# Spectral mixer on Trainium2: inverse transform laid out by image, its last stage on eight 32x64 tiles

## The chip, the cores and the metric

One core of a Trainium2 chip runs the whole kernel in one launch. The metric is device time in microseconds, the median of the runs shown. The engines are TensorE (PE), VectorE (DVE), ScalarE (ACT), GpSimd (POOL) and SyncE (SP), which here only issues transfers.

## The reference, cut to what matters

Input: x of shape (2, 64, 64, 384): two images, 64 rows (h), 64 columns (w), 384 channels. Four layers of the same kind follow each other; the second one is wrapped in a layer norm and followed by a two-layer token MLP with a second layer norm.

```python
xf = rfft2(x, axes=(1, 2))                   # 64 x 33 complex frequencies
o1 = act(complex_linear(xf, w1) + b1)        # 8 blocks of 48 channels; relu, or gelu in layer 1
o2 = complex_linear(o1, w2) + b2
o2 = softshrink(o2, 0.01)                    # layers 0, 2, 3
y  = irfft2(o2, s=(64, 64)) + x
# layer 1: ln -> the same with xk = xf[:, :32, :32], the rest zero -> + x -> ln -> gelu MLP -> + residual
```

Layers 0, 2 and 3 keep all 64 x 33 frequencies ("full" layers); layer 1 (the "norm" layer) keeps 32 x 32.

## The kernel before, in words

The work is done in 32 blocks, numbered g: layer g // 8, 48 channels each, so block g of a layer has one of its 8 channel groups. Two blocks are a unit (96 channels), which is what SP loads and stores; three buffers `xs` hold units. Partition of `xs` is (image, w). Blocks run in three segments: 0 to 7 (layer 0), 8 to 15 (layer 1, then the token MLP) and 16 to 31 (layers 2 and 3). Within a segment the stages of neighbouring blocks overlap, in an order written out by hand, in slots t: a full block has 9 slots (groups of 6 or 8 frequency slots), a norm block 4.

Stages of a block:
- `f1` (L479): transform along w, on 64x64 tiles of the array, three calls of 32 matmuls per block. Its input `xn` is turned by POOL (L1160). ACT copies the results into `z` (L726), four pieces per call.
- `f2` (L509): transform along h, ACT copies it into `zf` (L744). `m1` and `m2` (L527, L541): the two mixing matmuls, with ACT's activation `h` (L769) between them. In full layers DVE clamps and subtracts the result of `m2` into `u` (L931, L937), four subtractions per slot, one for each image and real or imaginary part.
- `f5` (L570): inverse along h, six calls (k = 0 to 5) per block, bank 5 of the PSUM alone, ACT copies it into `v` (L790).
- `f6` (L592): inverse along w, eight calls per block, each for 8 rows of the image: two matmuls with all 128 partitions of `v` (real or imaginary, frequency, image) as the contraction, 64 output columns each, 384 moving columns. The basis is zero where the image of the row isn't that of the output. DVE adds the result to the residual in `xs` (L954), 128x384 at a time, and in layer 0 takes `bn_stats` of every row there (L974), of 96 channels on odd blocks and of 48 on the last two.

Frequency 32, the last of the 33, needs only its real part, and frequency 0 needs no imaginary one: `f5` reads `u` shifted by one frequency for the imaginary half, so that frequency 32 lies where frequency 0's imaginary part would. For the norm layer two memsets on POOL (L1232) clear that place.

Order in slot t of block g on PE, full layers (L607): m1(g, t-1), f2(g, t), one f6 call (rows t+1 of block g-2; at t = 8 row chunk 0 of block g-1), f1(g+1) at t = 0, 3, 6, f5(g-1) at t = 2 to 7, m2(g, t-1). ACT (L804) and DVE (L1008) have orders to match. Each engine runs its own order strictly; they meet in semaphores. `f6` waits for `v_ready` (all six parts of `v`) and `res_ready` (the adds that free its bank). `m2` waits for `h_ready` and for the subtractions of the group two before it. At a segment's end PE finishes the rest without new blocks (L643 to L654).

SP stores a unit in four parts of 16 rows for each image when `res_ready` tells that both blocks' rows are there (L370), and then loads the next unit into the buffer. ACT and POOL issue no transfers.

Of the kernel before, what the change touches and what calls it, by code (L numbers as in the profile page):

```python
# [33 lines left out]
PIECES = ((0, 0), (0, 1), (1, 1), (1, 0))  # L34
ROWCHUNK = 8
# [5 lines left out]
AHEAD = 3  # L41
# [5 lines left out]
C_ID, C_D5, C_D5H, C_D6, C_COLS = [C_SIGN + SIGNS + P * n for n in range(5)]  # L47
# [11 lines left out]
class Layer:  # L59

    def __init__(self, index, kh, forward, inverse, act, shrink, norm):
        self.index, self.kh, self.forward, self.inverse = index, kh, forward, inverse
        self.act, self.shrink, self.norm = act, shrink, norm
        self.full = kh == SIDE
        self.spread = 2 * BATCH if self.full else BATCH
        self.first_rows = 1 if self.full else 0
# [47 lines left out]
def drains(g, k):  # L114

    last = [b for _, b in SEGMENTS if g < b][0]
    return g == last - 1 or g == last - 2 and k >= layer_of(g).first_rows


ROW_CHUNKS = [(g, k) for g in range(LAYERS * BLOCKS) for k in range(ROWCHUNKS)]  # L120


def row_bank(g, k):
    return 1 if drains(g, k) and k % 2 else 0


def rows_to_clear(g, k):

    n = ROWCHUNKS * g + k
    earlier = [m for m in range(n) if row_bank(*ROW_CHUNKS[m]) == row_bank(g, k)]  # L130
    return earlier[-1] + 1 if earlier else 0
# [63 lines left out]
def build(nc, x, consts, spectral, lncols, ln1, cols, w1, w2, b2, out):  # L195
    with ExitStack() as ctx:
# [24 lines left out]
        power = sb("power", [P, 1])  # L221
        eps = sb("eps", [P, 1])
# [4 lines left out]
        with ExitStack() as scope:  # L227
# [10 lines left out]
            u = sb("u", [P, 2, BLOCK, SPAN + BATCH])  # L238
# [3 lines left out]
            v = sb("v", [P, 2, SIDE, BLOCK])  # L242
# [31 lines left out]
        F1_BANKS, M2_BANKS, F6_BANKS = (0, 1), (4, 7), (6, 0)  # L274
        F2_BANK, M1_BANK, F5_BANK = 2, 3, 5
        LAST_BANKS = (F5_BANK, M1_BANK)
# [9 lines left out]
        f5_done, f6_done = sem("f5_done"), sem("f6_done")  # L286
        z_ready, zf_ready, h_ready = sem("z_ready"), sem("zf_ready"), sem("h_ready")
        clamped, u_ready, v_ready = sem("clamped"), sem("u_ready"), sem("v_ready")
        res_ready, gap_clear, u_clear = sem("res_ready"), sem("gap_clear"), sem("u_clear")
# [22 lines left out]
        TURN_AT = 8  # L312

# [5 lines left out]
        def residual(g, first, rows):  # L319

            n = g % 2
            return xs[buffer_of(g // 2)][:, first:first + rows, n * BLOCK:(n + 1) * BLOCK]
# [154 lines left out]
        def _(pe):  # L477

            def f1(g, k):  # L479
# [17 lines left out]
                if leads(g) and g and k == 1:  # L497
                    pe.wait_ge(res_ready, ROWCHUNKS * g)
                for c in range(CHAN):
# [41 lines left out]
            def m2(g, t):  # L541
# [9 lines left out]
                if L.full:  # L551
                    for c in range(size):
# [17 lines left out]
            def f5(g, k, bank=F5_BANK, reuse=1):  # L570
# [3 lines left out]
                if k == 0:  # L574
# [5 lines left out]
                    if L.norm and g % BLOCKS < 2:  # L580
                        pe.wait_ge(u_clear, 2)
                if n >= reuse:
                    pe.wait_ge(v_ready, n + 1 - reuse)
                for c in range(CHAN):
                    for a in range(2):
                        mm = pe.matmul(ps[a * SIDE:(a + 1) * SIDE, bank, c * SIDE:(c + 1) * SIDE],  # L586
                                       u[:, g % 2, k * CHAN + c, BATCH * a:BATCH * a + SPAN],
# [4 lines left out]
            def f6(g, k):  # L592

                n = ROWCHUNKS * g + k
                if k == 0:
                    pe.wait_ge(v_ready, CHUNKS * (g + 1))
                clear = rows_to_clear(g, k)
                if clear:
                    pe.wait_ge(res_ready, clear)
                rows = slice(k * ROWCHUNK, (k + 1) * ROWCHUNK)  # L600
                for a in range(2):
                    mm = pe.matmul(ps[a * SIDE:(a + 1) * SIDE, F6_BANKS[row_bank(g, k)], 0:ROWCHUNK * BLOCK],  # L602
                                   basis(C_D6 + a * SIDE, SIDE), v[:, g % 2, rows, :].rearrange("p h c -> p (h c)"),
                                   start=True, stop=True)
                mm.then_inc(f6_done, 1)

            def spectral(first, last):  # L607
# [3 lines left out]
                for g in range(first, last):  # L611
                    L = layer_of(g)
                    for t in range(L.n):
# [4 lines left out]
                        rows = [r for r in rows_at(g, t) if r[0] >= first]  # L618
                        ahead = at_slot(L.f1_at, t) if g + 1 < last else []
                        behind = at_slot(L.f5_at, t) if g > first else []  # L620
                        if not L.full:
                            for r in rows[0:1]:
                                f6(*r)
                        f2(g, t)
                        if L.full:
                            for r in rows:
                                f6(*r)
                            for k in ahead:
                                f1(g + 1, k)
                        for k in behind[0:1]:  # L630
                            f5(g - 1, k)
                        if not L.full:
                            for r in rows[1:]:
                                f6(*r)
                            for k in ahead:
                                f1(g + 1, k)
                        for k in behind[1:]:
# [3 lines left out]
                        elif g > first:  # L641
                            m2(g - 1, layer_of(g - 1).n - 1)
                g = last - 1  # L643
                m1(g, layer_of(g).n - 1)
                for k in range(L.first_rows, 4):
                    f6(g - 1, k)
                m2(g, layer_of(g).n - 1)
                f6(g - 1, 4)
                for k in range(CHUNKS):
                    if k < 3:  # L650
                        f6(g - 1, 5 + k)
                    f5(g, k, LAST_BANKS[k % 2], 2)
                for k in range(ROWCHUNKS):
                    f6(g, k)  # L654
# [69 lines left out]
        def _(act):  # L724
# [53 lines left out]
            def m2(g, t):  # L778
# [5 lines left out]
                for b in range(BATCH):  # L784
                    part = slice(SIDE + b * HALF, SIDE + (b + 1) * HALF)
                    act.activation(u[HALF:SIDE, g % 2, :, start + b:start + size:BATCH],
                                   ps[part, bank, 0:size // BATCH * BLOCK].rearrange("p (s c) -> p c s", c=BLOCK),
                                   ACT.Copy).then_inc(u_imag, 1)

            def f5(g, k, bank=F5_BANK):  # L790

                act.wait_ge(f5_done, CHUNKS * g + k + 1)
                if k == 0 and g >= 2:
                    act.wait_ge(f6_done, ROWCHUNKS * (g - 1))
                act.activation(v[:, g % 2, :, k * CHAN:(k + 1) * CHAN],
                               ps[:, bank, :].rearrange("p (c h) -> p h c", h=SIDE), ACT.Copy,
                               scale=layer_of(g).inverse).then_inc(v_ready, 1)

# [5 lines left out]
            def spectral(first, last):  # L804
# [5 lines left out]
                for g in range(first, last):  # L810
                    L = layer_of(g)
                    for t in range(L.n):
# [3 lines left out]
                        if L.full:  # L816
                            for k in late:
# [5 lines left out]
                        if not L.full:  # L823
                            for k in late:
                                f1(g + 1, k, PIECES[2:4])
# [6 lines left out]
                        for k in behind[0:1]:  # L832
                            f5(g - 1, k)
                        if not L.full:
                            for k in ahead:
                                f1(g + 1, k, PIECES[0:1])
                        for k in behind[1:]:
                            f5(g - 1, k)
                        if not L.full:
                            for k in ahead:  # L840
# [496 lines left out]
```

## Time and profile before

| | us |
|---|---|
| median of 3 runs (2064.65 to 2067.0) | 2065.68 |
| span of the profiled execution, first to last instruction | 2057.0 |
| median less span (launch and end) | 8.7 |
| PE busy, share of the span | 93% |
| DVE, ACT, POOL busy | 57%, 49%, 21% |

The page gives the profiled execution by its span alone; its own time from outside is not shown, so the median stands beside it. The segments lie in the span as follows: blocks 0 to 7 from 28 to 357 us, blocks 8 to 15 to 631 us, the token MLP to about 1460 us, blocks 16 to 31 to the end.

How to read it: a group of matmuls is told by its line. An fp32 matmul has two LDWEIGHTS and two MATMUL records. A busy time is the union of the records; the chain of waits cuts the same time into pieces that don't overlap. "issue" is time for which the profile shows no waiting.

### The profile page before, as it was taken

What the parts mean: (1) busy time and instruction counts of PE and PEld (TensorE: products, weight loads), DVE (VectorE), ACT (ScalarE), POOL (GpSimd) and SP (SyncE); (2) the same over time, 40 slices, a digit from 0 to 9 for tenths busy, and PEclk for the clock granted to TensorE, in tenths of its full rate; (3) what the DMA queues carried; (4) which work ended last, traced back from release to release, by engine and by line L of the source; (5) the groups of instructions that cost most, each with busy time, mean ns of one, the idle gap of its engine ahead of it and who ended that gap; (6) DMA issues with size and microseconds to landing.
All of it is one profiled execution on the core that took longest, in us unless ns stands there. A gap on an engine that the chain in (4) does not pass through costs nothing.

```text
span 2057.0 us, 68971 instructions
## 1 busy us (share of the span) xinstructions
PE 1919.2 (93%) x31104; PEld 1570.9 (76%) x31104; DVE 1173.7 (57%) x2480; ACT 1008.7 (49%) x1644; POOL 435.4 (21%) x425
## 2 busy tenths in 40 slices
PE   4999995698998999999999999999899999999996
PEld 3777772576776999999999999999777777777774
DVE  3687887977855433333333333332377767677675
ACT  3766545576753333333333333333466666665652
POOL 3212104965631000000000000000221211221200
PEclk9999997799999999999999999999999999999998
DMA  9425738307434111111111111114532573557314
GB/s 164 100 49 85 129 62 142 55 4 129 114 86 122 32 31 31 31 31 31 31 31 31 31 31 31 31 31 73 94 53 49 87 127 80 84 99 126 60 40 96
DMA packets 299701, 141.05 MB, mean 69 GB/s; under 512 B 275760, under 2 KB 298032, under 8 KB 299440
## 3 DMA queue, kind: packets, MB, share of 16 engines
q1 hardware_dynamic: 299440, 137.08, 36.2%
q8 instruction: 224, 3.67, 0.8%
q14 instruction: 37, 0.30, 0.1%
HBM read 74.14 MB, written 62.91 MB: 67 GB/s over the span
## 4 chain that ended last, share of the span: by engine, by line
PE 80%; DVE 9%; SPq 3%; ACT 2%; issue 2%; POOL 2%; DMA 1%; DVEq 0%; POOLq 0%; ACTq 0%
PE ps L693 20%; PE ps L678 19%; PE ps L586 8%; PE ps L523 8%; PE ps L537 7%; PE ps L602 6%; PE ps L555 5%; PE ps L504 4%; DVE u L937 3%; DVE st L974 2%; SPq L357 1%; DVE xs L962 1%; PE ps L565 1%; DMA wraw<-in_w 1%; PE ps L663 1%
## 5 line engine op out<-in xcount | busy, mean ns | idle before, releaser
L1086 DVE TENSOR_TENSOR gl<-g,gh 128x512 fp32r<-128x512 f32 x192 | 156.8, 816 | 476.3 <-ACT gh L872 476.3
L937 DVE TENSOR_TENSOR u<-ps,clamp 64x192 f32<-64x192 f32 (+1 forms) x864 | 378.1, 438 | 27.7
L869 ACT ACTIVATE g<-ps,colp 128x512 f32<-128x512 f32 x192 | 132.3, 689 | 529.1 <-PE ps L678 529.1
L523 PEld LDWEIGHTS ps<-const,z 128*48 128x48 f32 x8384 | 266.0, 124 | 134.9 <-issue 128.6
L732 ACT ACTIVATE z<-ps 64x512 f32<-64x512 f32 x366 | 234.9, 642 | 155.1 <-PE ps L504 148.2
L523 PE MATMUL ps<-const,z 128*48 128x64 f32 (+1 forms) x8384 | 270.3, 217 | 10.2 <-issue 5.3
L1173 POOL COPY xn<-xs 128x512 f32<-128x512 f32 x144 | 152.0, 1096 | 535.8 <-PE ps L504 343.9
L693 PE MATMUL ps<-w2h,gh 128*128 128x384 f32 x768 | 261.9, 341 | 0.0
L693 PE MATMUL ps<-w2h,gl 128*128 128x384 f32 x768 | 258.6, 337 | 0.0
L693 PE MATMUL ps<-w2l,gh 128*128 128x384 f32 x768 | 257.5, 335 | 0.0
L586 PEld LDWEIGHTS ps<-const,u 128*64 128x64 f32 x6144 | 206.7, 139 | 52.2 <-issue 25.7
L537 PE MATMUL ps<-zf,w 112*64 112x512 f32 (+1 forms) x992 | 244.2, 566 | 1.3 <-ACT zf L758 0.9
L602 PE MATMUL ps<-v,const 128*64 128x384 f32 x1024 | 216.1, 500 | 22.5 <-DVE xs L962 20.2
L586 PE MATMUL ps<-const,u 128*64 128x64 f32 x6144 | 220.0, 225 | 15.2 <-DVE u L942 7.6
L678 PE MATMUL ps<-mth,w1h 128*128 128x512 f32 x576 | 224.9, 390 | 4.0 <-DVE mtl L1074 4.0
L775 ACT ACTIVATE h<-ps,w 113x512 f32<-113x512 f32 (+1 forms) x248 | 162.7, 656 | 133.3 <-PE ps L537 130.8
L678 PE MATMUL ps<-mth,w1l 128*128 128x512 f32 x576 | 228.0, 396 | 0.0
L678 PE MATMUL ps<-mtl,w1h 128*128 128x512 f32 x576 | 227.6, 395 | 0.0
L931 DVE TENSOR_SCALAR clamp<-ps 128x384 f32<-128x384 f32 (+1 forms) x216 | 112.6, 521 | 181.6 <-PE ps L555 180.7
L504 PEld LDWEIGHTS ps<-const,xn 64*64 64x64 f32 x6144 | 110.0, 146 | 105.7 <-issue 77.9
L504 PE MATMUL ps<-const,xn 64*64 64x64 f32 x6144 | 124.3, 234 | 61.1 <-POOL xn L1173 23.5
L555 PE MATMUL ps<-w,h 113*64 113x96 f32 x3168 | 173.7, 248 | 7.4 <-ACT h L775 5.0
(70 smaller groups left out, 2463.4 us busy)
## 6 DMA issues: line engine op xcount, KB each, us to landing
after<-xs SPq DMA_DIRECT2D x96, 384.0 KB, 5.4
xs<-after SPq DMA_DIRECT2D x94, 384.0 KB, 8.8
after<-om SPq DMA_DIRECT2D x32, 384.0 KB, 4.3
out<-xs SPq DMA_DIRECT2D x32, 384.0 KB, 5.5
xm<-after SPq DMA_DIRECT2D x30, 384.0 KB, 6.3
xs<-in_x SPq DMA_DIRECT2D x24, 384.0 KB, 8.4
wstage<-in_spectral SPq DMA_DIRECT2D x16, 210.0 KB, 5.8
xs<-in_x SPq DMA_DIRECT2D x4, 768.0 KB, 11.9
```

The source lines that it names most:

```text
L504: mm = pe.matmul(ps[j * SIDE:(j + 1) * SIDE, banks[b], c * SPAN:(c + 1) * SPAN], xn[rows, slot, first + j, :], const[rows, C_D1:C_D1 + SPA ...
L523: mm = pe.matmul(ps[a * SIDE:a * SIDE + BLOCK, F2_BANK, n * L.kh:(n + 1) * L.kh], z[:, g % 2, slot, :], basis(col + a * SIDE, L.kh), start ...
L537: mm = pe.matmul(ps[rows, M1_BANK, 0:width], w[unit % 2][0:MIX, g % 2, rows], zf[0:MIX, n % 2, 0:width], start=True, stop=True)
L555: mm = pe.matmul(ps[b * SIDE:(b + 1) * SIDE, bank, p * PAIR:(p + 1) * PAIR], h[0:ROWS, n % 2, c * SIDE:(c + 1) * SIDE], mix[0:ROWS, g % 2, ...
L586: mm = pe.matmul(ps[a * SIDE:(a + 1) * SIDE, bank, c * SIDE:(c + 1) * SIDE], u[:, g % 2, k * CHAN + c, BATCH * a:BATCH * a + SPAN], basis( ...
L602: mm = pe.matmul(ps[a * SIDE:(a + 1) * SIDE, F6_BANKS[row_bank(g, k)], 0:ROWCHUNK * BLOCK], basis(C_D6 + a * SIDE, SIDE), v[:, g % 2, rows ...
L678: mm = pe.matmul(ps[:, MM1_BANKS[n % 2], :], a[:, at], b[r][:, k, :], start=k == 0 and m == 0, stop=k == KC - 1 and m == 2)
L693: mm = pe.matmul(ps[:, MM2_BANKS[j], 0:CHANNELS], a[:, n % 4, part], b[:, at], start=n == 0 and m == 0, stop=n == HC - 1 and m == 2)
L732: act.activation(to, data, ACT.Copy, scale=layer_of(g).forward).then_inc(z_ready, 1)
L775: act.activation(h[0:ROWS, n % 2, 0:width], ps[0:ROWS, M1_BANK, 0:width], L.act, bias=w[g // 2 % 2][0:ROWS, g % 2, READY_BIAS:W_ALL]).then ...
L937: dve.tensor_tensor(u[to, g % 2, :, start + b:start + size:BATCH], whole, limited, ALU.subtract).then_inc(u_ready, 1)
L1086: dve.tensor_tensor(gl[:, n % 4, :], g[:, n % 2, :], gh[:, n % 4, :], ALU.subtract).then_inc(g_low, 1)
```

## The change

`u` and `v` get the image as an outer index and the channels in two halves of 24 (TWO): `u[h part, parity, image, t, half, frequency]`, `v[..., image, row, t]`. The partition of `v` becomes (real or imaginary, channel half, frequency), four groups of 32. `f6` becomes two bursts of 32 rows per block, each on four banks: in step 0 all four 32-partition groups times two images run, each on its own 32x64 tile of the array; step 1 adds the other part (imaginary for real) into the same banks, after a semaphore `f6_half` that the last matmul of step 0 raises. Burst 0 of block g-1 stands at slot 8 of block g, burst 1 of block g-2 at slot 1 (both at slot 0 of the norm blocks). `f1` moves to slots 2, 4, 6, and `f5` to 2, 3, 4, 5, 6, 6 with two banks. Frequency 32 gets its own tile `last`, four small subtractions, a small `f5_last` (two matmuls at slot 2 of the next block, one DVE operation), and four transfers that ACT issues at the head of slot 7, each of 64 partitions x 96 bytes into one partition of `v`; burst 0 waits for them. The POOL memsets go.

```diff
-        self.f1_at = [0, 3, 6] if self.full else [0, 1, 2]
-        self.centre_at = [0, 0, 1, 2, 2, 3]
-        self.f5_at = [2, 3, 4, 5, 6, 7] if self.full else [1, 1, 2, 2, 3, 3]
+        self.f1_at = [2, 4, 6] if self.full else [1, 2, 3]
+        self.centre_at = [0, 1, 1, 2, 3, 3]
+        self.f5_at = [2, 3, 4, 5, 6, 6] if self.full else [1, 1, 2, 2, 3, 3]
-def rows_at(g, t):
+def bursts_at(g, t):
     if not layer_of(g).full:
-        return [(g - 2, 2 * t), (g - 2, 2 * t + 1)]
-    if t == layer_of(g).n - 1:
-        return [(g - 1, 0)]
-    return [(g - 2, t + 1)] if t < ROWCHUNKS - 1 else []
+        return [(g - 2, r) for r in range(BURSTS)] if t == 0 else []
+    return {1: [(g - 2, 1)], layer_of(g).n - 1: [(g - 1, 0)]}.get(t, [])
+STATS_AT = {0: (0, 1), 2: (2,), 3: (3,), 4: (4,), 5: (5,), 6: (6,), 7: (7,)}
+        BURST_BANKS, LAST_BURST_BANKS = (*F1_BANKS, *F5_BANKS), (M1_BANK, *M2_BANKS, F1_BANKS[0])
...
+            def f5_last(g):
+                pe.wait_ge(last_ready, 2 * BATCH * full_before(g + 1))
+                bank = last_bank(g)
...
+                for b in range(BATCH):
+                    mm = pe.matmul(ps[b * SIDE:(b + 1) * SIDE, bank, LAST_AT:LAST_AT + BLOCK],
+                                   basis(C_D5 + SIDE, SIDE), last[:, g % 2, b, :], start=True, stop=True)
+                mm.then_inc(last_done, 1)
...
+            def f6(g, r):
...
+                if r == 0:
                     pe.wait_ge(v_ready, CHUNKS * (g + 1))
+                    if layer_of(g).full:
+                        pe.wait_ge(v_whole, LAST_MOVES * full_before(g + 1))
+                    if g + 1 == last:
+                        pe.wait_ge(res_ready, ROWCHUNKS * g)
+                    elif layer_of(g).full:
+                        pe.wait_ge(z_ready, z_before(min(g + 3, last)))
+                elif g + 1 == last:
+                    pe.wait_ge(res_ready, ROWCHUNKS * g + 1)
+                else:
+                    pe.wait_ge(res_ready, ROWCHUNKS * g + 4)
+                for step in range(2):
+                    if step:
+                        pe.wait_ge(f6_half, BURSTS * g + r + 1)
+                    for n, bank in enumerate(burst_banks(g, r)):
+                        part, half = n // 2, n % 2
+                        a = part ^ step
+                        quadrant = slice((2 * a + half) * HALF, (2 * a + half + 1) * HALF)
+                        rows = slice(r * BURST_ROWS + part * BURST_PART, r * BURST_ROWS + (part + 1) * BURST_PART)
+                        for b in range(BATCH):
+                            mm = pe.matmul(ps[b * SIDE:(b + 1) * SIDE, bank, 0:BURST_PART * TWO],
+                                           const[quadrant, column:column + SIDE],
+                                           v[quadrant, g % 2, b, rows, :].rearrange("p h c -> p (h c)"),
+                                           start=step == 0, stop=step == 1)
+                    mm.then_inc(f6_done if step else f6_half, 1)
...
+            def place_last(g):
+                act.wait_ge(v_ready, CHUNKS * (g + 1))
+                act.wait_ge(last_kept, full_before(g + 1))
+                for b in range(BATCH):
+                    for j in range(2):
+                        row = SIDE + j * HALF
+                        act.dma_start(v[row:row + 1, g % 2, b], turned_last[b * SIDE:(b + 1) * SIDE, g % 2, j * TWO:(j + 1) * TWO]
+                                      ).then_inc(v_whole, 16)
...
+                        if start + size > SPAN:
...
+                            dve.tensor_tensor(last[to, g % 2, b, :], whole, limited, ALU.subtract).then_inc(last_ready, 1)
...
+            def f6(g, r):
...
+                dve.wait_ge(f6_done, BURSTS * g + r + 1)
+                for n, bank in enumerate(burst_banks(g, r)):
+                    to = residual(g, r * BURST_ROWS + n // 2 * BURST_PART, n % 2)
+                    dve.tensor_tensor(to, ps[:, bank, 0:BURST_PART * TWO].rearrange("p (h c) -> p h c", c=TWO),
+                                      to, ALU.add).then_inc(res_ready, 1)
...
-            pool.wait_ge(f5_done, CHUNKS * BLOCKS)
-            for n in range(2):
-                pool.memset(u[0:SIDE, n, :, SPAN:], 0.0).then_inc(u_clear, 1)
```

## Rows read from the trace of the kernel before

**Rows 1.** The page: busy time of the engines; the chain that ended last, by line.

```profile
PE 1919.2 (93%) x31104; PEld 1570.9 (76%) x31104; DVE 1173.7 (57%) x2480; ACT 1008.7 (49%) x1644; POOL 435.4 (21%) x425
...
PE ps L693 20%; PE ps L678 19%; PE ps L586 8%; PE ps L523 8%; PE ps L537 7%; PE ps L602 6%; PE ps L555 5%; PE ps L504 4%; DVE u L937 3%; DVE st L974 2%; SPq L357 1%; DVE xs L962 1%; PE ps L565 1%; DMA wraw<-in_w 1%; PE ps L663 1%
```

**Rows 2.** Busy time by stretch (us, then each engine): a block of layer 0, one with statistics, one of layer 2, a norm block.

```profile
93.83:128.34 34.51, 34.51 (x850) 25.85 (x848) 24.81 (x56) 22.02 (x37) 8.30 (x12) 1.00 0.01 3
128.34:163.71 35.37, 35.00 (x848) 25.88 (x844) 33.68 (x113) 22.08 (x36) 6.45 (x6) 1.00 0.47 96
1570.84:1605.41 34.57, 34.57 (x850) 25.88 (x848) 24.85 (x54) 22.09 (x36) 6.38 (x6) 1.00 0.51 102
432.70:460.71 28.01, 27.68 (x818) 21.21 (x816) 25.75 (x30) 21.33 (x35) 21.92 (x18) 1.00 0.02 4
```

**Rows 3.** Chain of waits, pieces of blocks 20 and 30 (start, us, what, records).

```profile
1612.91 0.93 PE ps L586 x32
...
1616.26 0.65 PE ps L602 x4
1616.90 1.09 PE ps L504 x64
1617.99 1.08 PE ps L586 x32
1619.08 0.66 PE ps L555 x16
1619.74 0.86 PE ps L537 x4
...
1993.13 0.67 PE ps L523 x24
```

**Rows 4.** Groups of PE by shape: f5 and f6 (busy, mean ns of a record, idle before).

```profile
L586 PE MATMUL ps<-const,u 128*64 128x64 f32 x6144 | 220.0, 225 | 15.2 <-DVE u L942 7.6 <-issue 3.0 <-ACT v L795 2.9
...
L602 PE MATMUL ps<-v,const 128*64 128x384 f32 x1024 | 216.1, 500 | 22.5 <-DVE xs L962 20.2 <-ACT v L795 2.1
```

**Rows 5.** Timeline of ACT, the same slots (start, us, what, idle before).

```profile
1618.06 1.30 ACT L732 ACTIVATE z<-ps 64x512 f32<-64x512 f32 x2 [1.16 <-PE ps L504]
1619.38 0.60 ACT L795 ACTIVATE v<-ps 128x512 f32<-128x512 f32 x1
1620.01 0.63 ACT L732 ACTIVATE z<-ps 64x512 f32<-64x512 f32 x1
1620.66 0.69 ACT L775 ACTIVATE h<-ps,w 113x512 f32<-113x512 f32 x1
```

**Rows 6.** Issues of SP by line, ns min/median/max: the smallest ones.

```profile
L392 SPq DMA_DIRECT2D wraw<-in_w x6: 327/328/432, 60.9 to 83.5; - x6
L464 SPq DMA_DIRECT2D lncol<-in_lncols x1: 437/437/437, 60.0 to 60.0; - x1
```

**Rows 7.** The same: a load of a unit's rows, four parts of two images each.

```profile
L357 SPq DMA_DIRECT2D xs<-after x96: 592/1981/3574, 236.4 to 1897.8; - x96
```

**Rows 8.** Transfers: KB each and median us from issue to landing.

```profile
const<-in_consts SPq DMA_DIRECT2D x1, 32.0 KB, 1.8
lncol<-in_lncols SPq DMA_DIRECT2D x1, 8.0 KB, 4.8
```

**Rows 9.** Groups of DVE by shape: subtractions, residual adds, row statistics.

```profile
L937 DVE TENSOR_TENSOR u<-ps,clamp 64x192 f32<-64x192 f32 x576 | 282.3, 490 | 18.5
...
L962 DVE TENSOR_TENSOR xs<-ps,xs 128x384 f32<-128x384 f32 x256 | 141.5, 554 | 54.7 <-PE ps L602 49.3
...
L974 DVE BATCH_NORM_STATS2 st<-xs 128x6 f32<-128x96 f32 x192 | 33.1, 246 | 0.8
```

**Rows 10.** Timeline of the end: last f6 calls, adds and stores.

```profile
2037.65 6.09 PE L602 MATMUL ps<-v,const 128*64 128x384 f32 x32 [0.70 <-ACT v L795]
...
2038.57 1.20 DVE L962 TENSOR_TENSOR xs<-ps,xs 128x384 f32<-128x384 f32 x2 [4.74 <-PE ps L602]
...
2039.80 12.46 SPq L375 DMA_DIRECT2D out<-xs  x8
```

More of the change, by code:

```diff
@@ L34 @@
 PIECES = ((0, 0), (0, 1), (1, 1), (1, 0))
+BURST_ROWS, BURST_PART = 32, 16
+BURSTS = SIDE // BURST_ROWS
 ROWCHUNK = 8
@@ L111, in imag_of, with segment_of, full_before @@
     return sum(BATCH for g, _ in GROUPS[:count] if layer_of(g).norm)
[L114 to L131, printed above, removed]
+def segment_of(g):
+    return [segment for segment in SEGMENTS if segment[0] <= g][-1]
+def full_before(g):
+    return sum(layer_of(n).full for n in range(g))
 def shrunk_before(g):
@@ L551, in m2 @@
                 if L.full:
+                    if t == LAST_SLOT and g > segment_of(g)[0]:
+                        f5_last(g - 1)
                     for c in range(size):
@@ L590, in f5 @@
                 mm.then_inc(f5_done, 1)
-            def f6(g, k):
-                n = ROWCHUNKS * g + k
-                if k == 0:
+            def f6(g, r):
+                first, last = segment_of(g)
+                column = C_D6 if layer_of(g).full else C_D6 + SIDE
+                if r == 0:
                     pe.wait_ge(v_ready, CHUNKS * (g + 1))
[L597 to L605, printed above, removed]
+                    if layer_of(g).full:
[22 more added lines that the diff above has]
+                    mm.then_inc(f6_done if step else f6_half, 1)
@@ L617, in spectral @@
                             m1(g - 1, layer_of(g - 1).n - 1)
-                        rows = [r for r in rows_at(g, t) if r[0] >= first]
+                        bursts = [r for r in bursts_at(g, t) if r[0] >= first]
                         ahead = at_slot(L.f1_at, t) if g + 1 < last else []
@@ L621, in spectral @@
                         if not L.full:
[L622 to L627, printed above, removed]
                             for k in ahead:
                                 f1(g + 1, k)
[L630 to L634, printed above, removed]
+                        f2(g, t)
+                        for r in bursts[0:1]:
+                            f6(*r)
+                        if L.full:
                             for k in ahead:
                                 f1(g + 1, k)
-                        for k in behind[1:]:
+                        for k in behind:
                             f5(g - 1, k)
@@ L816, in spectral @@
                         if L.full:
+                            if t == L.f5_at[-1] + 1 and g > first:
+                                place_last(g - 1)
                             for k in late:
@@ L831, in spectral @@
                                 f1(g + 1, k, PIECES[0:2])
-                        for k in behind[0:1]:
+                        else:
+                            for k in ahead:
+                                f1(g + 1, k, PIECES[2:4])
+                        for k in behind:
                             f5(g - 1, k)
[L834 to L840, printed above, removed]
-                                f1(g + 1, k, PIECES[1:2])
                         if L.norm and t:
@@ L926, in m2 @@
                 if L.full:
+                    if t == LAST_SLOT and g > segment_of(g)[0]:
+                        f5_last(g - 1)
                     pairs = size // BATCH
```

204 lines of the change are left out of this document (122 added, 82 removed).

## The prediction, made before the changed kernel ran

> **What bounds the kernel now.** I read the page first. PE is busy for 1919 of 2057 us and the chain that ended last is almost all PE [rows 1]. The token MLP's two lines hold 39% of it; the change doesn't touch them. f6 (L602) holds 6%, f5 8%, f2 8%. The busy share is a mean over stages, so I read single blocks next. In a clean full block PE is busy for all of its 34.5 us, DVE for 24.8, ACT for 22.1; in a block of layer 0 with row statistics DVE is up to 33.7 of 35.4; in a norm block PE has 27.7 and DVE 25.8 of 28.0 us [rows 2]. So PE's own work sets the pace of the full layers, with DVE just behind it where there are statistics and in the norm layer. The chain's pieces give the price of each stage on PE without overlap: one f6 call 0.65 us, f5 0.93, m2 0.66, m1 0.86, f2 of six slots 0.67, f1 1.09 [rows 3]. f6 is 8 x 0.65 = 5.2 us of each block. Most blocks away from the ends of a segment run like this.
>
> **What tiles cost and give.** f5's 32 records take 0.93 us on two tiles; f1's 64 records of the same 64 columns take 1.09 on four. That is 0.93 for twice as many records plus 0.16, and the f5 behind it takes 1.08, again 0.15 more [rows 3]. So four tiles run side by side, and each change of the tile shape costs 0.15 us. A f6 call streams 384 columns with two records per tile: 0.325 us a record. A record itself lasts about 0.49 without waits (the mean of 500 ns holds some slow ones) [rows 4], so a result is ready 0.16 us after its stream ends.
>
> **The bursts.** A burst has 16 matmuls in two steps of eight, one for each tile. If all eight run side by side it streams for 2 x 0.325 = 0.65, plus 0.05 for starting eight. Step 1 waits for the end of step 0: 0.16 for the last results, and some 0.12 for the semaphore and for loading weights that could not be loaded ahead, an estimate from the 0.15 of a shape change, which is a drain of the same kind. A burst then costs 0.15 + 0.70 + 0.28 + 0.70 + 0.15 = 1.98 us, two of them 3.96 against 5.2: 1.24 us less per full block. The trace shows no 32-row tile, so bounds: if nothing is paid between the steps 1.7 a burst (-1.8 per block); if only four of the eight tiles run at once each step is 1.35 and a burst 3.3 (+1.4 per block). I take 1.98, because f1 shows full use of all tiles there are.
>
> A page of the Trainium skill speaks against this. "TensorE: Matmul & The Clock Gate", section "Part 3: Packing small matmuls — row/col tiling", says that matmuls start and end in strict program order. By that rule the second record of a tile would hold back the next tile, and a step would take 2.9 us where I take 0.70. Were it so in f1, its 64 records could not end in 1.09 us; it is a rival below.
>
> **f5_last and the split subtractions.** f5_last is four records of 48 columns; m2's 16 of 96 take 0.66 [rows 3], so about 0.1 on PE. Net of f6 and this: -1.14 per full block. DVE gets four more small subtractions in one slot and one small copy, about 0.7 us per block between 64x192's 0.49 and nothing [rows 9]; it has 9.7 us to spare in a clean block [rows 2]: free. New write patterns in u (runs of four words in place of every second word) could make the 0.49 us shorter or longer; DVE is not the pace there: free. Two banks for f5 take away a wait that is small already (idle before f5 15.2 us in all, little of it for v) [rows 4]. The POOL memsets lie beside other work: nothing.
>
> **The four transfers on ACT.** Here the change pays. ACT issues them at the head of slot 7, after its last v copy, and everything behind them on ACT's queue comes later: one z piece and, above all, h for m2(6). PE at that point: from the end of the last f5 it has m2 0.66, m1 0.86, f2 0.67 = 2.19 us until it wants that h. ACT, by rows of the same kind: v done about 0.8 after f5 ends (a start 0.2 after it, then 0.60), z 0.63, h 0.69 = 2.15 [rows 5]. So the cover is 0.04 us and the time of the four issues falls on PE in full. Nothing before gives ACT's issue time. SP's smallest are 0.33 (wraw) and 0.44 us (lncol, 128 short rows) [rows 6]; these have 64 short rows. Bounds: 0.15 (half the smallest row, since the rows are half as many) and 2.0, what an issue of SP takes with its queue full [rows 7]. I take 0.40, nearest to lncol in kind: 1.6 us per block. Then the landing: small transfers landed after 1.8 us on an idle queue and 4.8 behind others [rows 8]. Between ACT's last issue and burst 0 PE does m2, m1, f2 and waits for h: z 0.63 + h 0.69 + m2 0.66 + m1 0.7 + f2 0.67 = 3.35 us. At 1.8 it is hidden; at 4.8 it costs 1.5. I take hidden.
>
> **Who waits for the bursts.** DVE adds four tiles of 0.55 us in a row [rows 9], 2.2 us, and a m2 group behind them. At slots 8, 0 and 1 DVE has two such bursts and three groups of m2, each four subtractions of 0.33 to 0.49 us (six slots have three quarters of the elements) and a clamp of about an add's 0.5: some 10.5 us, and PE about 10; m2 may run two groups ahead and f1 has moved from slot 0 to 2, where banks 0 and 1 are free just in time. Nothing in clean blocks. In blocks of layer 0 with statistics the new order puts 16 bn_stats (0.17 us each: 33.1 for 192) into slot 0: 2.7 us more, of which I count 2 as stall, in blocks 3, 5 and 7.
>
> **Norm blocks.** Both bursts stand in slot 0, with a m2 between them (32 records, about 0.9 like f5's); burst 1 waits for the adds of burst 0, 2.2 us: a stall of 1.3. Then 2 x 1.98 + 1.3 = 5.3, what f6 costs now. DVE is at 92% of such a block anyway. I count 0 per block, between -2 and +2.
>
> **Ends.** Segment 3 ends with f6, then SP's eight stores of 1.56 us each and a landing [rows 10]. Now place_last stands bare in front of f6: 1.6 + 1.8 = 3.4 us, and the first two adds come 0.9 later than now (a whole burst first). Fewer waits in the drain of the block before give 1.3 back: +3. The end of layer 0 is a DVE queue (statistics), 0; the end of the norm layer gains about 1.5 because two f6 calls no longer stand between the f5.
>
> **The sum.** Layers 2 and 3: 16 x -1.14 + 15 x 1.64 = +6.4; end +3. Layer 0: 8 x -1.14 + 7 x 1.64 + 3 x 2 = +8.4, of which part is covered by DVE; I take +5. Norm 0 and -1.5. Together +13 us against the span of 2057.0; the median of the runs shown lies 8.7 above that span. So 2065.7 + 13 = 2079.
>
> **The rivals.** (A) The transfers are cheap or hidden: issue 0.15, or ACT's queue goes on beside it. Then the place costs at most 0.64 per block, the net is -0.5 to -1.1, and layers 0, 2 and 3 give 24 x -0.5 to -1.1, with the same ends and statistics stalls down to 2: 2041 to 2060, about 2048. For it: 64 rows only, an empty queue. Against: no issue under 0.33 in the trace. The point from which it decides is four issues in 1.1 us. (B) Issuing is slow while SP's queue is full: 2.0 us each in the blocks where SP loads, every second one, for 11 blocks: 11 x 6.4 = +70 on the forecast, 2150; half of that at 1.2 us, 2110. For it: SP's median of 1.98. Against: that may be the filling of its own ring. (C) The eight tiles don't run side by side, four do: 4 x 0.65 = +2.6 per block over my sum in 32 blocks, +83, 2160. So the change would not do what it says. Against: f1's four tiles. (D) Records start in strict order, so a tile's second record holds back the next tile: a step takes (8 + 1) x 0.325 = 2.93 in place of 0.70, 4 x 2.2 = +9 per block, 32 blocks, +285, 2364. Only f1's row bears on it, against it. Slower by another way than my forecast are B, C, D; A ends on the other side.
>
> **Chances.** Forecast 0.41 (its own range 2065 to 2098), A 0.36, B 0.13, C 0.07, D 0.03. 0.2% is 4 us, about what a measurement of this kernel tells from no change. Faster by more: A's most, 0.32. Within it: 0.12, the upper end of A and the lower of the forecast. Slower: 0.56. The range for 8 in 10 reaches from A's 2040 over the forecast to B's lower case with the landing bare, 2125; it leaves out half of B, C, D and A's low end (all bounds at their good end, 24 x -1.4: 2032).
>
> **What would show it.** In the profile after: per burst 32 records of 128 rows' worth in 32x64 tiles, from first to last start about 1.7 us; f6 below 140 us of PE. ACT's 96 DMA issues at 0.3 to 0.5 us; a new wait of PE for ACT's h of about 1.6 us once per full block; hardly any wait of f6 for a DMA outside the last block. Clean full block 34.5 -> 35.0 us; if it is 33.4 to 34, A holds; if f6 keeps over 3 us a burst, C or D. The prediction is wrong if the norm blocks change by over 2 us each, or if DVE turns into the releaser of PE in clean blocks.

## The result, and the profile of the changed kernel

The changed kernel takes 2148.65 us (median, 2144.1 to 2157.1), the kernel before beside it 2065.16 (2061.5 to 2067.0): ratio 1.0404, 95% interval 1.0373 to 1.0435. I had said 2079, at most 2125. The direction was right, the size was not: +83.5 us where +13 was forecast.

The page of the changed kernel, its span 2155.3 us: the first two lines answer to those of [rows 1], the third is the group of m2 on PE:

```profile
PE 1925.4 (89%) x32224; PEld 1572.0 (73%) x32224; DVE 1162.0 (54%) x2608; ACT 1004.2 (47%) x1644; POOL 442.8 (21%) x423
...
PE ps L740 19%; PE ps L725 19%; PE ps L544 8%; PE ps L622 8%; PE ps L558 7%; PE ps L578 6%; PE ps L653 5%; PE ps L525 5%; ACTq L854 2%; DVE xs L1032 2%; SPq L376 1%; DVE xn L1069 1%; PE ps L710 1%; DVE u L1000 1%; DVE st L1047 1%
...
L578 PE MATMUL ps<-w,h 113*64 113x96 f32 x3168 | 182.5, 255 | 56.1 <-ACT h L822 49.3
```

PE does 6 us more than before, and the span is 98 us longer: PE waits. Half of the wait has a name, ACT's h in front of m2 (L578), 49.3 us where it was 5.0 before. The same by stretch (columns as in [rows 2]): a clean block of layer 0, one with statistics, a block with loads, a clean block, and the 15 blocks 16 to 30 together:

```profile
100.22:136.59 36.37, 33.77 (x886) 25.54 (x886) 24.34 (x60) 22.12 (x36) 8.38 (x12) 1.00 0.02 4
136.59:174.43 37.84, 33.96 (x886) 25.82 (x886) 35.25 (x124) 22.12 (x36) 6.43 (x6) 1.00 0.55 113
1770.91:1812.63 41.72, 36.84 (x886) 27.35 (x886) 24.22 (x60) 22.06 (x36) 6.34 (x6) 0.92 0.90 160
1971.32:2007.69 36.37, 33.76 (x886) 25.54 (x886) 23.86 (x59) 22.11 (x36) 8.35 (x12) 1.00 0.02 4
...
1504.13:2083.32 579.19, 521.08 (x12958) 392.51 (x12958) 354.69 (x844) 327.85 (x535) 101.75 (x121) 0.96 0.43 75
```

The same 15 blocks, and two of them (24 with loads, 25 with stores alone), in the kernel before:

```profile
1475.56:1993.86 518.30, 507.07 (x12458) 384.34 (x12460) 361.46 (x772) 327.11 (x535) 101.61 (x121) 1.00 0.48 83
...
1746.81:1783.62 36.81, 35.15 (x850) 26.58 (x848) 24.85 (x54) 22.02 (x37) 8.33 (x12) 1.00 0.54 83
1783.62:1818.18 34.56, 34.56 (x850) 25.87 (x848) 24.87 (x54) 22.05 (x36) 6.41 (x6) 1.00 0.50 102
```

A clean block went from 34.5 to 36.37 us, a block with loads from 36.8 to 41.7, and in the latter the granted clock fell to a mean of 0.92 of full. So there are two losses, one in each block and one beside SP's transfers. The first stands in the chain of waits of block 28, slots 6 to 8 (start, us, what):

```profile
1997.13 0.61 ACT v L843
...
1997.76 0.47 ACTq L854
1998.23 0.03 issue
1998.26 0.62 ACTq L854
...
2000.17 0.05 issue
2000.22 0.63 ACT z L779
...
2000.88 0.70 ACT h L822
2001.57 0.04 issue
2001.62 0.88 PE ps L578 x16
...
2003.82 0.92 PE ps L653 x16
2004.73 0.04 issue
2004.77 0.91 PE ps L653 x16
```

Four issues on ACT's queue reach from 1997.76 to 2000.17, 2.42 us, and z, h and m2 come behind them. The burst, whose price was the least certain, is as worked out: its two steps take 0.92 + 0.04 + 0.91 = 1.87 us. The individual records of this burst show its first eight starts within 0.05 us of each other, and the second record of each tile 0.37 us later: eight tiles side by side. Issue durations (ns min/median/max) and landing, by line:

```profile
L854 ACTq DMA_DIRECT2D v<-turned_last x96: 470/618/1522, 90.2 to 2131.9; - x96
...
DMA to landing us min/median/max: 1.7/1.9/7.2
```

The group of f6 on PE (busy, mean ns of a record, idle before); it was 216.1 us busy in [rows 4]:

```profile
L653 PE MATMUL ps<-v,const 32*64 32x384 f32 x2048 | 132.7, 570 | 37.8 <-DVE xs L1032 15.8 <-issue 13.3 <-ACT v L843 0.7
```

### The profile page after: what moved, and what is told of

Read it like the earlier page. It is cut to its first block, busy times and chain, and to the rows that moved or that the text cites. A ratio compares the mean times of both kernels' runs of the same rounds, so it can differ in the third digit from the quotient of the medians.

```text
span 2155.3 us, 71501 instructions
## 1 busy us (share of the span) xinstructions
PE 1925.4 (89%) x32224; PEld 1572.0 (73%) x32224; DVE 1162.0 (54%) x2608; ACT 1004.2 (47%) x1644; POOL 442.8 (21%) x423
## 4 chain that ended last, share of the span: by engine, by line
PE 79%; DVE 7%; issue 4%; ACT 3%; SPq 3%; ACTq 2%; POOL 1%; DMA 0%; DVEq 0%; POOLq 0%
PE ps L740 19%; PE ps L725 19%; PE ps L544 8%; PE ps L622 8%; PE ps L558 7%; PE ps L578 6%; PE ps L653 5%; PE ps L525 5%; ACTq L854 2%; DVE xs L1032 2%; SPq L376 1%; DVE xn L1069 1%; PE ps L710 1%; DVE u L1000 1%; DVE st L1047 1%
## 5 line engine op out<-in xcount | busy, mean ns | idle before, releaser
L544 PEld LDWEIGHTS ps<-const,z 128*48 128x48 f32 x8384 | 276.3, 128 | 142.3 <-issue 134.2
L1000 DVE TENSOR_TENSOR u<-ps,clamp 64x192 f32<-64x192 f32 (+2 forms) x864 | 365.1, 423 | 24.6
L544 PE MATMUL ps<-const,z 128*48 128x64 f32 (+1 forms) x8384 | 283.7, 222 | 17.1 <-issue 12.1
L558 PE MATMUL ps<-zf,w 112*64 112x512 f32 (+1 forms) x992 | 257.9, 592 | 5.0 <-issue 2.0
L578 PE MATMUL ps<-w,h 113*64 113x96 f32 x3168 | 182.5, 255 | 56.1 <-ACT h L822 49.3
L622 PE MATMUL ps<-const,u 128*64 128x64 f32 x6144 | 215.0, 227 | 15.6 <-issue 11.0
L622 PEld LDWEIGHTS ps<-const,u 128*64 128x64 f32 x6144 | 198.2, 141 | 22.2 <-issue 13.2
L578 PEld LDWEIGHTS ps<-w,h 113*64 113x64 f32 x3168 | 145.7, 140 | 92.3 <-ACT h L822 57.1
```

What stands on the lines that cost most here:

```text
L544: mm = pe.matmul(ps[a * SIDE:a * SIDE + BLOCK, F2_BANK, n * L.kh:(n + 1) * L.kh], z[:, g % 2, slot, :], basis(col + a * SIDE, L.kh), start ...
L558: mm = pe.matmul(ps[rows, M1_BANK, 0:width], w[unit % 2][0:MIX, g % 2, rows], zf[0:MIX, n % 2, 0:width], start=True, stop=True)
L578: mm = pe.matmul(ps[b * SIDE:(b + 1) * SIDE, bank, p * PAIR:(p + 1) * PAIR], h[0:ROWS, n % 2, c * SIDE:(c + 1) * SIDE], mix[0:ROWS, g % 2, ...
L1000: dve.tensor_tensor(modes(g, to, b, start, size), whole, limited, ALU.subtract).then_inc(u_ready, 1)
```

## Experiments: the transfers

The first four runs separate the transfers from the new order of PE's work.

```diff
e1   -    place_last(...)   and the waits on v_whole
e2   -    for b, for j: act.dma_start(v[row, g % 2, b], ...)        4 x 64 rows of 96 B
     +    for j:        act.dma_start(v[row, g % 2], turned_last[:, g % 2, j])   2 x 128 rows
e3   as e2, but pool.dma_start behind POOL's six turns of a block
e4   kernel before, plus 4 x act.dma_start(spare, turned_last) at the head of slot 7
```

**e1**, expected:

> The changed kernel without the four transfers that ACT issues per full block and without the waits for them (frequency 32 is still computed, but not placed). Theory A (the issues stand on PE's path through ACT's queue, about 2.5 us per full block, and the gaps let TensorE's clock fall): a clean full block goes from 36.4 to about 33.9 us, 24 blocks give 60 us, the clock and the fetch stalls behind the gaps up to 30 more: 2055 to 2090 us, no PE wait for h over 0.5 us. Theory B (the bursts and the new order of the slots cost the time, the transfers little): over 2130 us, clean block still about 36.

**e2**, expected:

> The same data placed by two transfers of 128 rows of 96 bytes in place of four of 64. Theory A: an issue costs about 0.65 us by itself, whatever its rows, so 1.3 us less per full block, 31 us in all, and shorter gaps let the clock fall less often: 2095 to 2120 us. If the issue's cost goes by rows (twice as long each), or by theory B: no change, 2140 to 2155.

**e3**, expected:

> The two transfers issued by POOL, in its idle time after the sixth turn of a block; ACT issues none. Theory A: like the run without transfers, 2055 to 2090 us, if they land before PE reaches burst 0, some 5 us after the last v copy. If POOL issues late or they land late, PE waits for them in front of f6 and each us late costs 24 us in all. Theory B: 2130 or more.

**e4**, expected:

> The kernel before, with four transfers of 64 rows of 96 bytes added on ACT at the head of slot 7 of 22 full blocks, into memory that nothing reads (in HBM). Nothing waits for them but the program's end. Theory A: the issues alone delay h by 2.5 us; here PE has f5 in slot 7 as well, 0.9 us of cover, so 1.6 to 2.5 us per block, 35 to 55 us, and some clock loss: 2100 to 2140 us. Theory B: within 10 us of before, 2065 to 2075.

Measured, with the length of blocks from one eviction of f2(0) to the next (load blocks: 20 to 28 with even numbers in the kernel before and in e4, 19 to 27 with odd numbers otherwise):

```
                     us (median)  ratio [95% interval]      clean   load blocks
before               2065                                   34.51   35.4 to 36.8
after                2148.65      1.0404 [1.0373, 1.0435]   36.37   41.5 to 42.8
e1 no transfers      2075.12      1.0052 [1.0032, 1.0073]   34.15   36.8 to 41.0
e2 two by ACT        2118.38      1.0242 [1.0196, 1.0288]   35.08   40.1 to 43.0
e3 two by POOL       2102.39      1.0180 [1.0147, 1.0213]   34.15   40.2 to 43.4
e4 before plus four  2107.44      1.0202 [1.0166, 1.0237]   35.51   36.9 to 40.6
```

The transfers cost 73.5 us of the 83.5 (2148.65 - 2075.12); e1, e2 and e4 lie in the ranges expected. Clean blocks say how: 34.15 us without, 35.08 with two issues, 36.37 with four, and 34.15 again when POOL issues them, which has nothing behind them that PE wants soon. So what costs is not data on its way (landing 1.9 us) but ACT's time ahead of h. The kernel before, given four such issues whose data nobody uses, loses 42 us as well. But e3 is no cure, and came out 12 us above its range: it keeps its gain in clean blocks, and in load blocks slot 6 grows from 5.3 to between 8.8 and 12.1 us and slot 8 from 3.8 to up to 8.3. In slot 8 it is the landing, as in block 21: the two transfers, issued at 1681.85 and 1682.38, have their last packet done at 1687.3, and the burst comes late and at half clock:

```profile
1688.94 3.29 PE L653 MATMUL ps<-v,const 32*64 32x384 f32 x32 [2.07 <-issue]
```

What slot 6 loses is told under what stops PE.

## Experiments: where ACT issues, and when SP loads

e1 left 10 us that the new order costs, though its clean blocks are shorter than before. In blocks 16 to 30 all of it stands beside SP's transfers: the five load blocks take 199 us where the kernel before took 181. SP's issues over block 23 of the changed kernel (timeline):

```profile
1770.08 12.32 SPq L394 DMA_DIRECT2D after<-xs  x8
...
1787.13 13.84 SPq L376 DMA_DIRECT2D xs<-after  x8
```

In the kernel before the stores came two by two and the loads after the last of them:

```profile
1714.15 26.60 SPq L375 DMA_DIRECT2D after<-xs  x8
...
1744.24 13.28 SPq L357 DMA_DIRECT2D xs<-after  x8
```

A burst finishes 32 rows at once, so all stores are issued by slot 3 and the loads start in slot 4 of the same block (16 us after its start); before, they started 32 us after it, in slot 8. Four runs, and one that only moves ACT's issues:

```diff
e5, e6, e7   +  sp.wait_ge(f2_done, groups_before(2 * unit + 4) + 1)      ahead of load_unit(unit + 3)
             e5 on e1, e6 on the changed kernel, e7 on e3
e8   slot 7 of ACT:  -  place_last, z, h, zf     +  z, h, place_last, zf
```

**e5**, expected:

> The changed kernel without the transfers (the last frequency is not placed, so that part of the result is left out), and SP issues the 14 us of loads of the unit three ahead one block later: when block 2*unit+4 begins, not as soon as the stores have landed. Without that delay it took 2075.1 us, with clean blocks of 34.15 us and load blocks of 36.8 to 41.0 us, in which the loads lie over slots 2 to 6. Theory L (what the new order still costs is that the earlier stores let the loads fall on the stretches with f1 and f5): load blocks 35.5 to 37.0 us, 2055 to 2064 us, below the kernel before. Rival M (the load blocks are long wherever the loads lie, since DMA traffic slows PE all the same): 2072 to 2078 us.

**e6**, expected:

> The changed kernel whole, with the same delay of the loads. Theory L: its load blocks go from 42 us to 38 to 39 us (36.4 us clean plus about 2), so some 8 blocks by 3.5 us, -28: 2115 to 2128 us. Rival M: 2143 to 2152 us. Rival A2 (the four ACT issues are slow mainly because SP issues at the same time; the delay moves the loads off slot 7 too, or onto it): the h wait in load blocks would change from 3.2 us to 2.3 us or the other way, up to 5 us of the total.

**e7**, expected:

> The changed kernel with two transfers issued by GpSimd in place of four by ACT (2102.4 us), and the loads delayed. Theory L: the loads no longer hold back the landing of the small transfers before the burst nor lie over f1 and f5, load blocks from 40 to 43 us to 36 to 37 us: 2060 to 2078 us. Rival M: 2098 to 2105 us. Below 2065 it beats both kernels.

**e8**, expected:

> The changed kernel with ACT's four issues put behind its copy of h(6) and ahead of the eviction of f2(7), everything else as changed. If the 2.3 us of a block are ACT's issue time ahead of h, m2(6) no longer waits 2.34 us for h, 22 blocks by -2.3 is -50 us; the burst behind f2(7) then waits for transfers that start 0.7 us later: issues 2.47 + landing 1.8 us after h against f2(7) 0.65 us, some 3 us of wait in front of the burst. So theory I (the issue time decides, landing had cover to spare): 2100 to 2125 us. Rival N (landing had no cover to spare, the wait moves from h to the burst): 2145 to 2175 us, with PE waiting for a DMA before L653 in each block.

The late loads lie in blocks 20 to 28 with even numbers; these are the load blocks of e5 to e7 here.

```
                           us (median)  ratio [95% interval]      clean   load blocks
e5 no transfers, late      2081.77      1.0067 [1.0044, 1.0090]   34.15   37.3 to 38.6
e6 whole, late             2160.58      1.0442 [1.0411, 1.0473]   36.37   40.7 to 43.4
e7 two by POOL, late       2091.92      1.0128 [1.0105, 1.0150]   34.15   37.8 to 39.5
e8 four behind h           2151.13      1.0403 [1.0376, 1.0431]   35.80   41.3 to 45.2
```

My theory L was wrong as I had put it: with the loads one block later e5 and e6 came out no faster. The single load block got shorter, but the store block beside it now lost 1.1 us too (35.3 us), and a load from slot 0 on still covers the dense slots 2 to 4. The edit also holds back the loads of layer 0 and of the norm layer: in the profiled executions blocks 16 to 30 of e5 take 4.0 us less than those of e1 (531.4 and 535.4), layer 0 takes 6.9 more and the norm layer with the MLP 10.2 more, which was not taken apart. Only e7 gained, 10 us, and stays 14 above its range: its slot 6 is 5.3 us again and slot 8 at most 4.6, with the loads gone from there, while slot 2 grows from 4.6 to up to 8.6.

e8 moved the wait, as its rival said, but not to the place that it named. Chain of waits of a clean block:

```profile
1665.81 0.88 PE ps L558 x4
...
1666.78 0.47 ACTq L854
...
1668.59 0.62 ACTq L854
1669.20 0.05 issue
1669.25 0.50 ACT zf L799
...
1669.79 0.86 PE ps L558 x3
```

h(6) is in time, but zf(7) stands behind the issues now and m1(7) (L558) waits for it. Both places that were tried in ACT's queue between v and the burst have something behind them that PE wants within some 2 us.

## Experiments: what stops PE beside SP's transfers

In load blocks PE stops in the middle of a line, waiting for nothing that the profile shows. PE's timeline in block 23 of the changed kernel (idle before, and what ended it, in brackets):

```profile
1793.42 0.68 PE L525 MATMUL ps<-const,xn 64*64 64x64 f32 x29
1795.53 0.79 PE L525 MATMUL ps<-const,xn 64*64 64x64 f32 x35 [1.43 <-issue]
...
1799.69 0.44 PE L544 MATMUL ps<-const,z 128*48 128x64 f32 x9
1802.03 0.77 PE L544 MATMUL ps<-const,z 128*48 128x64 f32 x15 [1.89 <-issue]
1803.62 1.55 PE L578 MATMUL ps<-w,h 113*64 113x96 f32 x16 [0.83 <-ACT h L822]
```

The page lists a queue of kind "instruction":

```profile
q8 instruction: 233, 3.82, 0.8%
```

I set the landings of its packets (16384 bytes each) beside the ends of these stops; worked out from the packet records of the same block:

```
packet on q8 lands   PE's stop       stop ends after the landing
1787.17              -
1794.11              1794.10-1795.53   1.42
1800.50              1800.14-1802.03   1.53
```

Of the 16 stops of 0.7 us and more inside one line in the full layers of the changed kernel, 15 end 1.2 to 1.8 us after an instruction packet has landed (a window in which 10% of all moments fall). The kernel before has stops of that size too: in its blocks 16 to 30 they make 8.8 us in sum, in those of e1 18.1. Theory Q reads them so: PE has run through the instructions that it holds. How many it holds, no run here measured. The Trainium skill, "Runtime: NRT & Kernel Launch", section "Instruction fetch mechanics", says that each sequencer fetches 16 KiB blocks over a DMA queue of its own; the size agrees with the records. It calls the cost mostly hidden; here clean blocks show no such stop, and blocks with stores and loads do.

The test: put the loads where PE has few instructions (the two bursts of slots 8 and 1 are 64 long records), space the stores as before, and take half of the loads away. The waits of e9 to e12 stand in the full layers alone.

```diff
e9   on e3:   +  sp.wait_ge(f2_done, groups_before(2 * unit + 3) + 8)         ahead of load_unit(unit + 3)
e10  on e9:   +  sp.wait_ge(f2_done, groups_before(2 * unit + 3) + 2 * part)  ahead of the stores of parts 1 to 3
e11  e10's waits on e1     e12  e10's waits on the changed kernel
e13  on e1:   -  load_unit(unit + 3)     +  load_rows(unit + 3, b, part, PART_ROWS // 2)
```

**e9**, expected:

> Two transfers issued by GpSimd (2102.4 us without a delay of the loads, 2091.9 us with the loads at the start of block 2*unit+4). Now the loads begin once f2 of slot 7 of block 2*unit+3 has ended. Theory Q: PE stops in a load stretch because its next instructions arrive late beside the bulk traffic (in the traces so far each stop ends 1.3 to 1.65 us after an instruction packet has landed). The slots 7, 8, 0 and 1 hold few PE instructions (two bursts of 16 long matmuls each) and last 12.8 us, which covers nearly all of the 14 us of loads; pairs of blocks from 73.7 us (e7) to 70 to 71.5 us, 9 pairs: 2060 to 2075 us. Rival T (the stops belong to the traffic, wherever PE is): 2088 to 2095 us.

**e10**, expected:

> As the run before, and the four parts of a unit's stores are held two slots apart (parts 1, 2 and 3 until f2 of slots 1, 3 and 5 of block 2*unit+3 has ended), about as the kernel before issued them: 8 stores in 26 us there, 12 to 13 us in the changed kernel. Theory Q: the stops of 1 to 1.4 us a pair in the store stretch vanish too: pairs of 69 to 70 us, 2050 to 2068 us, 7 to 12 us under the run before. Rival T: the same time as the run before within 3 us.

**e11**, expected:

> The changed kernel without the transfers (the last frequency is not placed), with the loads at slot 7 and the stores spaced. It leaves nothing of the change but its order of PE work: clean pairs are 68.3 us against 69.1 us in the kernel before. Theory Q: 2045 to 2057 us, faster than before. Rival T: 2072 to 2082 us.

**e12**, expected:

> The changed kernel whole (four issues by ACT) with the same timing of loads and stores. Theory Q: what is left is the wait for h behind ACT's issues, 22 blocks by 2.3 us over the run without transfers, +50 us: 2095 to 2110 us. If ACT's issues are also slower beside SP's loads (up to 3.2 us a block, seen in the load blocks of the changed kernel) the loads at slot 7 come just behind them and the h wait stays at 2.3 us. Rival T: 2143 to 2155 us.

**e13**, expected:

> The changed kernel without the transfers (2075.1 us, load blocks 36.8 to 41.0 us against 34.15 us clean) and with only half the rows of each unit loaded three units ahead (half the bytes and packets; the other rows keep old data, so the result is not the transform of the input). Nothing else changed. Theory Q (PE stops once the instructions that it holds have run out while the next packet is held up behind bulk packets): the traffic behind a unit's stores is 7 us instead of 14 us, most stops vanish and not only half: blocks 19 to 27 with odd numbers 34.2 to 36.5 us, 2052 to 2063 us. Rival T (each microsecond of traffic slows PE by its share): half of the 5 us remains, 36.5 to 38 us a block, 2064 to 2070 us. Rival U (the stops have nothing to do with the loads): 2072 to 2078 us.

Load blocks are those of 20 to 28 with even numbers here, and for e13 those of 19 to 27 with odd ones.

```
                            us (median)  ratio [95% interval]      clean   load blocks
e9  two by POOL, slot 7     2078.37      1.0063 [1.0027, 1.0099]   34.15   35.6 to 37.1
e10 and stores spaced       2076.58      1.0050 [1.0025, 1.0075]   34.15   35.6 to 38.3
e11 no transfers, both      2069.49      1.0023 [0.9998, 1.0047]   34.15   35.3 to 38.5
e12 whole, both             2135.73      1.0351 [1.0300, 1.0402]   36.4    36.6 to 41.4
e13 half loads              2045.28      0.9903 [0.9868, 0.9937]   34.15   35.1 to 35.9
```

Where only the place of the loads changed, time moved as theory Q says: e9 is 24 us under e3 and 13.5 under e7 (its blocks 24 and 25 are 70.6 us together, as expected), though 3 us above my range. Spacing the stores gave nothing that can be told apart (-1.8 us), against my 7 to 12, so e10 and e11 missed their ranges by 9 and 12 us: that half of my reading fell. e13 halves the loads, and their blocks lose three quarters of their excess, not half (the five of e1 mean 39.7 us, here 35.5, over 34.15); in all it gained 30 us, 7 more than the end of my range. The stops of blocks 16 to 30 fall from 18.1 us in e1 to 4.0. Theories T and U are out. Blocks 24 and 25 of e13, then the 15 blocks together:

```profile
1738.04:1772.19 34.15, 33.77 (x886) 25.54 (x886) 24.33 (x60) 22.18 (x37) 8.34 (x12) 1.00 0.02 4
1772.19:1807.88 35.69, 34.39 (x886) 25.91 (x886) 24.35 (x60) 22.19 (x36) 6.39 (x6) 1.00 0.69 141
...
1465.92:1981.46 515.54, 500.47 (x12958) 379.39 (x12958) 355.56 (x844) 329.02 (x534) 101.51 (x121) 1.00 0.35 68
```

e12 missed its 2095 to 2110. Over e11 it loses 66 us, where 22 waits of 2.3 us make 50. In blocks 16 to 30 PE's idle time grows by 32.2 us, which is 14 such waits, and its busy time by 7.1; from block 31 on, where ACT's issues stand bare, 8.4 more are lost. The 7.1 us go with the clock: it is at its lower level (1.2 GHz) for 24 us of these blocks in e12 and for 7 in e11, by the clock records; for 51 us in the changed kernel, 17 in e1, 3 in e13 and none before. The granted clock of the 15 blocks is 0.96 in the changed kernel, 0.98 in e1 and e12, 1.00 in e9 and e13. These stretches come after such waits and stops, and in the timeline above m2 takes 1.55 us after its wait, not 0.83.

No version here beats the kernel before while it computes the whole result. e13 and e11 leave work out; e10 is the best whole one.

## Why the prediction failed, by its steps

The sum had two halves, and e1 sets them apart. For the transfers it held 22 x 1.64 + 3.4 at the end = 39.5 us; they cost 73.5. For the new order of PE's work it held the rest, -26.5; e1 is 10 slower than the kernel before. Both halves missed, by 34 and by some 36 us, and on the same side.

For blocks 16 to 30 the windows give the whole account. PE's work at full clock is 500.47 us (e13) against 507.07 before: -6.6, where I had forecast -1.14 for each of 15 (-17). The same work takes 521.08 - 500.47 = 20.6 more in the changed kernel, which is at the lower clock for 51 us of it, and idle time went from 11.2 to 58.1: +46.9. Of the 58.1 us, 30.9 are m2's waits for h and 22.5 stops with no releaser. Together +60.9, which is 579.19 - 518.30.

- **"A burst costs 1.98 us"** held: 1.87 and a change of tile shape. f6 came to 132.7 us (under 140 said). The strict order of starts and ends that the page "TensorE: Matmul & The Clock Gate" of the Trainium skill states in "Part 3: Packing small matmuls — row/col tiling" does not hold record by record, as rival D took it: eight first records start within 0.05 us, ahead of the eight second ones. Whether whole matmuls keep their order these records do not tell. Rivals C and D are out.
- **"-1.14 per full block"** failed: a clean block without transfers is 34.15, -0.36. PE is busy for 33.77 of it, 0.74 less than before, and stands for 0.38: 0.13 between the steps of each burst and 0.12 for h. The last shows in e1's chain, where slot 7 has only f2 beside h:

```profile
1782.68 0.89 PE ps L558 x4
1783.56 0.02 issue
1783.59 0.70 ACT h L820
1784.29 0.04 issue
1784.33 0.88 PE ps L578 x16
```

  h is made from m1's result and can't start before m1 ends, 0.76 us ahead of m2, and f2(7) fills 0.67 of them. I had set h behind v and z only. Behind this wait m2 takes 0.88 us, not 0.66. In the chain of block 20 of e1, set beside that of block 25 of the kernel before, f5 takes 0.16 us more in sum (6.04, not 5.88) and m1 0.19 (7.30, not 7.11), for which I had counted nothing.
- **"I take 0.40 for an issue"** failed. An issue took 0.47 to 0.62 us and the next began 0.03 later: 2.42 for four, beside my 1.6, and up to 3.3 beside SP's issues. It was inside my bounds of 0.15 to 2.0, but the nearest row by rows and bytes, SP's lncol at 0.44 [rows 6], was no guide to the engine. In clean blocks that is 2.22 us of loss for 1.64. These two steps explain 36.37 where I said 35.0, some 30 us of the 70 that the forecast missed, over the 22 blocks with transfers inside a segment.
- **"So the cover is 0.04"** was nearly right: of 2.42 us, 2.22 are on the path. v was done 0.63 us after f5 in the chain above, not 0.8.
- **What the sum lacked**, about as much again. Each term was the price in a clean block. The changed kernel's five load blocks take 5.8 us more than its clean one (mean 42.1 over 36.4); before, such a block took 1.7 more (mean of five 36.2 over 34.5), and in e1, without transfers, 5.6. I counted no cost for the earlier stores and loads, although SP's queue was one that the change moves work past. And I counted a wait as its length, not the clock that it costs.
- **Landing hidden**, right in clean blocks; in load blocks of e3, where nothing holds PE back ahead of the burst, it was not (7.1 us at most).
- **Rival B** gave 2150, and that it lies near the result is luck: issues of 2.0 us were never seen, the longest is 1.5, and four beside SP's issues took up to 0.9 us more than four alone, not 6.4. **Rival A** fell with the 2.42 us. Its point of decision, four issues in 1.1 us, was the right question.
- **Norm blocks, ends.** Norm layer and MLP together came out 4.7 us longer (forecast -1.5); of this, blocks 8 to 14 took 4.3 (220.5 us for 216.3), 0.6 each where I had 0. At the end ACT's issues stand bare, as forecast, but the bursts run at half clock after that wait, and each takes 3.3 us, not 1.98:

```profile
2130.08 2.41 ACTq L854 DMA_DIRECT2D v<-turned_last  x4
2133.84 0.36 PEld L653 LDWEIGHTS ps<-v,const 32*64 32x64 f32 x16 [4.58 <-issue]
2133.88 3.29 PE L653 MATMUL ps<-v,const 32*64 32x384 f32 x32 [4.47 <-issue]
...
2137.88 3.30 PE L653 MATMUL ps<-v,const 32*64 32x384 f32 x32 [0.72 <-DVE xs L1032]
```

  The tail from block 31 on grew by 8.8 us, +3 said, and layer 0 by 23.2, where I had +5; its blocks show the same two losses (a clean one 36.37 us), and I did not divide it further.

## What to carry to other kernels

A DMA issue is an instruction of the engine that issues it: put it on an engine whose queue holds nothing that the bottleneck wants soon, and price it there at 0.65 us each, up to 1.1 beside another engine's issues (four took 4.4 us in e4), not by its bytes. Sum a change over the kinds of blocks that the timeline has, not over the clean one: where the change finishes rows earlier, it also moves stores and loads. A wait on PE costs more than its length where the clock falls behind it.

## What the runs showed of the hardware that I had not expected

- Four small transfers by ACT (6 KB each) block its queue for 2.42 us; two of 12 KB cost a clean block 0.93 us, four of 6 KB 2.22. For the same bytes in all, the number of issues decides.
- PE stops for 0.8 to 3.7 us in the middle of a line of the changed kernel, ending 1.2 to 1.8 us after an instruction packet of 16 KB has landed, beside stores and loads at a DMA share of 0.9. The tie to the fetch of instructions is by time and by e9 and e13, and so argued, not shown; a run that changes PE's instruction count alone was not made.
- Halving the loads gains 30 us of 2075, more than the 27 (24 x 1.14) that I had forecast for the whole new order of PE's work. What the kernel before would gain by it was not run.
